# A fused cross-attention and FFN kernel: the maximum over the partitions by TensorE, first loads as units of the lists, new lists, and every second piece of w1 and w2 rounded by ScalarE

## The reference

```
n = layernorm(x)
q = quantized_linear(n, wq, bq)          # rows of n and rows of wq rounded to 127 levels by their own maximum
k = ctx @ wk.T + bk ; v = ctx @ wv.T + bv
o = softmax(q k.T / sqrt(32) + mask) v   # 16 heads of 32
x = x + quantized_linear(o, wo, bo)
n = layernorm(x)
h = gelu(quantized(n) @ quantized(W1).T * scales + B1)     # W1 and W2: one maximum over the WHOLE weight
x = x + quantized(h) @ quantized(W2).T * scales + B2
```

## Time and profile before

| what | us |
|---|---|
| median of three runs (lowest, highest) | 703.0 (701.41, 705.25) |
| the profiled execution, its own time | 699.67 |
| its span in the profile | 697.9 |
| PE busy | 639.8 (92%) |
| DVE busy | 475.1 (68%) |
| ACT busy | 462.5 (66%) |
| POOL busy | 219.0 (31%) |

### The profile page before, as it was taken

How to read it: one execution, slowest core, us unless ns; L and a number is a source line. 1 busy time by engine, 2 the same in 40 slices (tenths; PEclk the granted TensorE clock), 3 DMA queues, 4 the chain that set the end, 5 groups by cost and what they waited for, 6 DMA issues and landing times.

```text
span 697.9 us, 14934 instructions
## 1 busy us (share of the span) xinstructions
PE 639.8 (92%) x5168; PEld 475.6 (68%) x5168; DVE 475.1 (68%) x1173; ACT 462.5 (66%) x1158; POOL 219.0 (31%) x457
## 2 busy tenths in 40 slices
PE   2773996989999999999899999989999999999989
PEld 1562775857777687777777778767677776767644
DVE  4653884678667776778567563658577677878775
ACT  3241574658767776778578796668687867878812
POOL 0113330434071424235232433323424435221200
PEclk8896998999999999999999999999999999999999
DMA  9762596650605351353516352432533333232110
GB/s 307 273 92 58 65 263 129 157 157 19 84 24 98 94 75 27 58 105 23 132 10 113 79 66 23 71 75 33 59 97 67 79 49 61 40 58 41 39 38 23
DMA packets 80586, 58.67 MB, mean 84 GB/s; under 512 B 57984, under 2 KB 67968, under 8 KB 79872
## 3 DMA queue, kind: packets, MB, share of 16 engines
q1 hardware_dynamic: 80512, 57.72, 40.8%
HBM read 41.85 MB, written 3.68 MB: 65 GB/s over the span
## 4 chain that ended last, share of the span: by engine, by line
PE 72%; DVE 9%; DMA 9%; issue 5%; POOL 2%; ACT 2%; SPq 1%; DVEq 0%; POOLq 0%
PE ps_ring L1054 30%; PE ps_t L1088 11%; PE ps_ring L1160 7%; PE ps_s L1081 6%; PE ps_ring L1173 6%; PE ps_t L1100 5%; DMA rs_in<-row_sum 3%; PE ps_s L1149 3%; DMA oqT<-o_q 2%; PE ps_ring L1122 2%; PE ps_ring L1047 2%; DMA hT<-h_q 1%; DMA h<-in_wq 1%; DMA q_dram<-cols 1%; DVE cols L838 1%
## 5 line engine op out<-in xcount | busy, mean ns | idle before, releaser
L716 ACT ACTIVATE probs<-probs,neg_max 112x375 f32<-112x375 f32 x256 | 153.6, 602 | 42.7 <-DVE neg_max L867 42.1
L867 DVE CUSTOM_DVE_ANT_0 probs<-ps_s,mask_in 112x375 f32<-112x375 f32 x256 | 129.3, 545 | 60.0 <-PE ps_s L1081 51.8
L726 ACT ACTIVATE pT<-ps_t 125x336 f32<-125x336 f32 x256 | 110.2, 446 | 66.9 <-PE ps_t L1088 63.9
L1088 PEld LDWEIGHTS ps_t<-ident,probs 112*125 112x125 f32 x768 | 108.4, 189 | 40.2 <-issue 21.2
L1088 PE MATMUL ps_t<-ident,probs 112*125 112x112 f32 x768 | 120.5, 279 | 3.3 <-ACT pT L726 1.5
L1054 PE MATMUL ps_ring<-ctx_hi,wk_hi 128*128 128x376 f32 x256 | 91.9, 359 | 12.8 <-DVE ctx_lo L956 11.9
L1054 PE MATMUL ps_ring<-wv_hi,ctx_hi 128*125 128x512 f32 x192 | 80.5, 419 | 16.9 <-POOL ctx_lo L635 10.4
L1054 PE MATMUL ps_ring<-ctx_lo,wk_hi 128*128 128x376 f32 x256 | 86.8, 339 | 0.0
L1054 PE MATMUL ps_ring<-ctx_hi,wk_lo 128*128 128x376 f32 x256 | 86.8, 339 | 0.0
L635 POOL TENSOR_TENSOR ctx_lo<-ctx_in,ctx_hi 128x376 fp32r<-128x376 f32 x60 | 59.5, 997 | 74.3 <-ACT ctx_hi L694 52.8
L1054 PE MATMUL ps_ring<-wv_lo,ctx_hi 128*125 128x512 f32 x192 | 76.5, 398 | 0.0
(11 more groups left out here) (127 smaller groups left out, 1072.8 us busy)
## 6 DMA issues: line engine op xcount, KB each, us to landing
ctx_in<-in_ctxT SPq DMA_DIRECT2D x32, 375.0 KB, 5.0
h<-in_w2T SPq DMA_DIRECT2D x4, 1024.0 KB, 6.6
b_row<-in_w2T SPq DMA_DIRECT2D x4, 1024.0 KB, 7.3
x_in<-in_x SPq DMA_DIRECT2D x16, 224.0 KB
xres<-in_x SPq DMA_DIRECT2D x14, 256.0 KB, 2.9
out<-y SPq DMA_DIRECT2D x14, 256.0 KB, 2.3
mask_in<-in_mask SPq DMA_DIRECT2D x16, 164.1 KB, 3.7
w_q<-in_w1T SPq DMA_DIRECT2D x2, 1024.0 KB, 8.8
```

The lines of the kernel that those rows point to most:

```text
L716: nc.scalar.activation(probs[:, hd % SP_RING, :], probs[:, hd % SP_RING, :], ACT.Exp, scale=-1.0, bias=neg_max[:, b % 2, hd:hd + 1], accum ...
L726: nc.scalar.activation(pT[0:LR, hd % PT_RING, :], att_bank("T", b, hd)[0:LR, 0:LC * N], ACT.Copy).then_inc(pT_s, 1)
L867: nc.vector.tensor_tensor_reduce(out=probs[:, hd % SP_RING, :], in0=ps_s[hd % HG][0:N, 0:L], in1=mask_in[:, b % 2, :], scale=-1.0, scalar= ...
L1088: last = nc.tensor.transpose(bank[0:LR, lc * N:(lc + 1) * N], probs[:, hd % SP_RING, lc * LR:(lc + 1) * LR], ident[0:N, 0:N])
```

## The change

- **Maximum over the partitions.** POOL's `prepare` with its all-reduce goes. PE's new unit `w_max which.0` transposes the column of 128 maxima into one row (a matmul with the identity), DVE's new unit `w_max` reduces the row to one number, and PE's `w_max which.1` spreads it over the partitions (a matmul with a row of ones). DVE's step 5 reads it there. Both PE units take a bank of the ring.
- **Rounding.** Pieces m = 1 and m = 3 of w1 and of w2 are rounded by ACT (steps 7, 8, 11, 12 leave DVE's list and enter ACT's): ACTIVATE Identity with a scale and +constant, then with -constant. SP's loads into the buffers wait for ACT's semaphore where ACT frees them.
- **First loads.** They are units of SP's list. x comes first, then half of ctx and of wk, then wq; the bias rows come tens of units later. `mask_load 0.0` and `xres_load 0.0` stand behind `ctx_load 2.0` and `2.1`, no longer right behind the first weights.
- **Warm units** are of 4 matmuls in place of 8; 12 of them stand ahead of `k 0.0` in place of 2, and 3 more among the first work in place of 2. 24 in place of 12 stand in the last part.
- **All five lists are new**, with the same units otherwise. The last tile's lists on DVE and ACT are as before.

The lists up to the first heads, before and after (the rest is left out here; it differs by moves of some units, at most some thirty places):

```diff
 SP_UNITS
-w_load 0.0 prepare 0.0 0.1 0.2 x_load 0.0 ctx_load 0.0 0.1 prepare 0.3 0.6 mask_load 0.0 xres_load 0.0 prepare 0.8 w_load 0.1
-ctx_load 1.0 mask_load 1.0 w_load 0.2 0.3 xs_out 0.0 ctx_load 1.1 x_T 0.0 x_load 1.0 xs_in 0.0 ctx_load 2.0 2.1 xs_out 1.0 x_load
+x_load 0.0 ctx_load 0.0 load_wk 0.0 prepare 0.0 load_wq 0.0 load_wk 0.1 ctx_load 0.1 load_col 0.0 load_wv 0.0 prepare 0.1 load_wv
+0.1 load_col 0.1 prepare 0.2 load_wo 0.0 w_load 0.0 ctx_load 1.0 w_load 0.1 xs_out 0.0 ctx_load 1.1 prepare 0.3 w_load 0.2 x_load
+1.0 x_T 0.0 prepare 0.6 xs_in 0.0 w_load 0.3 ctx_load 2.0 mask_load 0.0 ctx_load 2.1 xres_load 0.0 load_row 0.0 prepare 0.8
...
 POOL_UNITS
-x_norm 0.0 x_quant 0.0 split 1.0 1.1 prepare 0.4 split 1.2 1.3 q 0.0 x_norm 1.0 split 2.0 2.1 x_quant 1.0 residual 0.0 split 2.2
+x_norm 0.0 split 1.0 x_quant 0.0 split 1.1 1.2 1.3 q 0.0 x_norm 1.0 split 2.0 2.1 2.2 x_quant 1.0 x_norm 2.0 split 2.3 residual
...
 ACT_UNITS
-split 0.0 0.1 0.2 w_hi 0.0 split 0.3 w_hi 0.1 k 0.0 w_hi 0.2 0.3 v 0.0 0.1 w_evac 0.0 v 0.2 w_evac 0.1 so 0.0 w_evac 0.2 split 1.0
-w_evac 0.3 0.4 0.5 0.6 split 1.1 k 0.1 0.2 w_evac 0.7 split 1.2 1.3 k 0.3 split 2.0 v 1.0 split 2.1 v 1.1 S 0.0 0.1 split 2.2 k
+split 0.0 0.1 w_hi 0.0 0.1 split 0.2 0.3 w_hi 0.2 k 0.0 0.1 0.2 w_evac 0.0 0.1 0.2 w_hi 0.3 w_evac 0.3 split 1.0 1.1 k 0.3 v 0.0
+split 1.2 v 0.1 split 1.3 v 0.2 w_evac 0.4 0.5 split 2.0 v 1.0 w_evac 0.6 split 2.1 w_evac 0.7 S 0.0 v 1.1 split 2.2 S 0.1 T 0.0
+prepare 0.7 k 1.0 prepare 0.8 S 0.2 k 1.1 S 0.3 T 0.1 prepare 0.11 S 0.4 0.5 T 0.2 so 0.0 split 2.3 v 1.2 T 0.3 S 0.6 T 0.4
+prepare 0.12 k 1.2 T 0.5 S 0.7 k 1.3 T 0.6 PV 0.0 S 0.8 0.9 T 0.7 S 0.10 0.11 split 3.0 T 0.8 0.9 S 0.12 PV 0.1 T 0.10 S 0.13 0.14
...
 DVE_UNITS
-w_lo 0.0 split 0.0 w_lo 0.1 split 0.1 0.2 w_rows 0.0 0.1 0.2 split 0.3 x_norm 0.0 w_lo 0.2 0.3 w_rows 0.3 0.4 prepare 0.0 w_rows
-0.5 x_quant 0.0 prepare 0.1 0.2 0.3 0.4 0.5 0.6 q 0.0 x_norm 1.0 prepare 0.7 S 0.0 prepare 0.8 x_quant 1.0 S 0.1 0.2 0.3 prepare
+split 0.0 w_lo 0.0 x_norm 0.0 w_rows 0.0 split 0.1 w_lo 0.1 split 0.2 0.3 x_quant 0.0 w_lo 0.2 w_rows 0.1 0.2 0.3 w_lo 0.3 w_rows
+0.4 0.5 prepare 0.0 0.1 x_norm 1.0 q 0.0 prepare 0.2 0.3 S 0.0 x_quant 1.0 prepare 0.4 S 0.1 w_max 0.0 S 0.2 0.3 prepare 0.5 0.6
...
 PE_UNITS
-warm 0.0 0.1 k 0.0 warm 0.2 v 0.0 0.1 warm 0.3 w_T 0.0 v 0.2 so 0.0 w_T 0.1 0.2 0.3 0.4 0.5 0.6 k 0.1 0.2 w_T 0.7 k 0.3 q 0.0 v
-1.0 S 0.0 v 1.1 k 1.0 v 1.2 S 0.1 T 0.0 0.1 k 1.1 1.2 T 0.2 0.3 S 0.2 T 0.4 PV 0.0 T 0.5 0.6 q 1.0 T 0.7 S 0.3 T 0.8 0.9 k 1.3 T
+warm 0.0 0.1 0.2 0.3 0.4 0.5 0.6 0.7 0.8 0.9 0.10 0.11 k 0.0 0.1 0.2 w_T 0.0 warm 0.12 w_T 0.1 0.2 warm 0.13 w_T 0.3 k 0.3 v 0.0
+0.1 0.2 q 0.0 w_T 0.4 warm 0.14 w_T 0.5 v 1.0 w_T 0.6 S 0.0 w_T 0.7 v 1.1 w_max 0.0 T 0.0 w_max 0.1 k 1.0 1.1 S 0.1 T 0.1 so 0.0 v
...
```

The functions:

```diff
-            def prepare(which, step):
-                if step == 4:
-                    pool.wait_ge(w_max, 2 * which + 1)
-                    nc.gpsimd.partition_all_reduce(w_all[:, which:which + 1], w_rs[:, 8 + which:9 + which], P,
-                                                   bass.bass_isa.ReduceOp.max).then_inc(w_max, 1)
...
+            def prepare(which, step):
+
+                stages, w = ((st_w1, w1_q), (st_w2, w2_q))[which]
+                m, rounding = (step - 5) // 2, (step - 5) % 2
+                stage, inv = stages[m % len(stages)], w_rs[:, 10 + which:11 + which]
+                if not rounding:
+                    act.wait_ge(round_ready, 2)
+                    act.wait_ge(w_inv, which + 1)
+                    if which == 1:
+                        act.wait_ge(w_in[12 + m], 16)
+                    nc.scalar.activation(stage, stage, ACT.Identity, scale=inv, bias=round_up[:]).then_inc(w_round_act, 1)
+                else:
+                    act.wait_ge(w_round_act, 2 * which + m // 2 + 1)
+                    nc.scalar.activation(w[:, :, :].rearrange("p k n -> p (k n)")[:, m * F:(m + 1) * F], stage, ACT.Identity,
+                                         bias=round_down[:]).then_inc(w_quant_act, 1)
...
-                        dve.wait_ge(w_max, 2 * which + 2)
-                        nc.vector.tensor_scalar(col[:], w_all[:, which:which + 1], 1.0 / LEVELS, None, ALU.mult).then_inc(w_col, 1)
+                        dve.wait_ge(w_max_all, which + 1)
+                        nc.vector.tensor_scalar(col[:], bank_of("w_max", which, 1)[:, 0:1], 1.0 / LEVELS, None, ALU.mult).then_inc(w_col, 1)
...
+            def w_max_part(which, i):
+                dve.wait_ge(w_max_T, which + 1)
+                nc.vector.tensor_reduce(w_one[:, which:which + 1], bank_of("w_max", which, 0)[0:1, 0:P], AX.X, ALU.max).then_inc(w_max_row, 1)
...
+            def w_max_unit(which, i):
+
+                if i == 0:
+                    pe.wait_ge(w_max, which + 1)
+                    bank = ring_bank("w_max", which, 0)
+                    nc.tensor.matmul(bank[0:1, 0:P], w_rs[:, 8 + which:9 + which], ident[:], start=True, stop=True).then_inc(w_max_T, 1)
+                else:
+                    pe.wait_ge(w_max_row, which + 1)
+                    bank = ring_bank("w_max", which, 1)
+                    nc.tensor.matmul(bank[:, 0:1], ones[0:1, :], w_one[:, which:which + 1], start=True, stop=True).then_inc(w_max_all, 1)
...
-WARM = 8
+WARM = 4
```

More of the change, by code:

```diff
@@ L43 @@
[L43 to L50, removed]
@@ new lines @@
+residual 2.0 x_quant 5.0 split 5.3 x_norm 6.0 y_norm 2.0 split 6.0 q 5.0 split 6.1 6.2 x_quant 6.0 split 6.3 7.0 residual 3.0
+x_norm 7.0 split 7.1 7.2 y_norm 3.0 split 7.3 y_quant 2.0 3.0 residual 4.0 q 6.0 x_quant 7.0 y_norm 4.0 split 8.0 8.1 8.2 q 7.0
+x_norm 8.0 x_quant 8.0 split 8.3 residual 5.0 split 9.0 9.1 y_norm 5.0 x_norm 9.0 split 9.2 y_quant 4.0 q 8.0 x_quant 9.0 split
+9.3 y_quant 5.0 residual 6.0 x_norm 10.0 split 10.0 10.1 10.2 y_norm 6.0 y_quant 6.0 split 10.3 q 9.0 x_quant 10.0 residual 7.0
@@ new lines @@
+12.12 12.13 x_norm 14.0 S 12.14 12.15 up 9.0 9.1 9.2 9.3 q 13.0 S 13.0 gather 10.0 h_absmax 9.0 o_quant 10.0 S 13.1 13.2 h_absmax
+9.1 S 13.3 h_absmax 9.2 9.3 x_quant 14.0 h_quant 9.0 out_proj 10.0 S 13.4 y_norm 10.0 S 13.5 13.6 13.7 y_quant 10.0 S 13.8 13.9
+13.10 13.11 down 9.3 S 13.12 13.13 x_norm 15.0 S 13.14 up 10.0 10.1 S 13.15 q 14.0 up 10.2 h_absmax 10.0 up 10.3 h_absmax 10.1
+10.2 10.3 h_quant 10.0 S 14.0 gather 11.0 o_quant 11.0 S 14.1 14.2 14.3 14.4 14.5 out_proj 11.0 S 14.6 14.7 y_norm 11.0 x_quant
@@ L192 @@
+1.16 1.17 1.18 h_T 13.0 13.1 warm 1.19 down 13.0 13.1 13.2 13.3 warm 1.20 1.21 1.22 1.23
 """
@@ L218 @@
 RING_USES = [use for use in turns(PE_UNITS)
-             if use[0] in ("w_T", "so", "q", "k", "v", "gather", "o_T", "out_proj", "y_T", "up", "h_T") or use[0] == "down" and use[2] == 0]
+             if use[0] in ("w_T", "so", "w_max", "q", "k", "v", "gather", "o_T", "out_proj", "y_T", "up", "h_T") or use[0] == "down" and use[2] == 0]
 RING_AT = {use: n for n, use in enumerate(RING_USES)}
@@ L665, in y_quant @@
                 nc.gpsimd.tensor_tensor(y[b % 2], y[b % 2], b2_row[:], ALU.add).then_inc(y_b2_s, 1)
-            units = {"prepare": prepare, "x_norm": x_norm, "split": split_lo, "x_quant": x_quant, "q": q, "residual": residual,
+            units = {"x_norm": x_norm, "split": split_lo, "x_quant": x_quant, "q": q, "residual": residual,
                      "y_norm": y_norm, "y_quant": y_quant}
@@ L1175, in down @@
                     last.then_inc(down_pe, 1)
-            units = {"w_T": w_T, "so": so, "q": q, "k": k_unit, "v": v_unit, "S": S, "T": T, "PV": PV, "gather": gather,
+            units = {"w_T": w_T, "so": so, "w_max": w_max_unit, "q": q, "k": k_unit, "v": v_unit, "S": S, "T": T, "PV": PV, "gather": gather,
                      "o_T": o_T, "out_proj": out_proj, "y_T": y_T, "up": up, "h_T": h_T, "down": down, "warm": warm}
```

338 lines of the change are left out of this document (174 added, 164 removed).

## The result

The kernel after takes 694.14 us (median of 4 runs, 691.96 to 695.85), the kernel before beside it 702.3 us (701.41 to 705.25): ratio 0.9875, 95% interval 0.9833 to 0.9917. It is faster by 1.2%, and not by the 4.0% of the forecast; 694 lies above the range. The profiled execution took 691.96 us, its span is 689.7.

The account below looks back on a forecast made before the run. TensorE's own work was taken as the bound from 200 to 660 us, with the loss in gaps before about 130 us. Terms -28.2 -6.5 +1.5 +1.1 +4 = -28.1 from 703.0 gave 675 us, range 664 to 687.

Parts of the forecast that it names:

- First loads, and TensorE up to S 0.0: Front: k 0.0 starts at about 16 us, first scores S 0.0 at 42 instead of 70.18, minus 28.2 us.
- The second stop: Before scores S 1.2 at 119.84 us: replacing the second all-reduce removes idle and slow scores, minus 6.5 us.
- The maximum itself: Two tiny matmuls and a DVE reduction per maximum cost 0.8 us each, plus 1.5 us for both.
- Rounding by ACT: Eight pieces add 16.4 us to ACT, of which a quarter shows, plus 4 us; DVE's saved 10.1 us count nothing.
- SP's queue: Row loads, mask 1 and xres move behind the first work on SP's list and are needed later: no cost.
- The rest of the lists and the tail: New orders of all 16 batches, same work, TensorE 98% busy: zero, bounds minus 10.6 and plus 10 us.
- The sum: All terms over the whole kernel: minus 28.1 us from the median of 703.0, giving 675 us.
- The condition named for being wrong: Middle of the kernel: the forecast is wrong if TensorE has over 20 us of idle there.
- TensorE's waits for ACT's copies: The forecast is wrong if these waits grow by over 10 us.
- (e): Rival: in every tile out_proj waits for the transposed oqT, 35 us over 13 tiles, 710 us; chance 0.03.
- (b): Rival: ACT becomes the bound in batches 0 and 1, its whole 16.4 us shows, 687 us; chance 0.13.
- (c): Rival: the new orders also remove the later idle of 10.6 us, 664 us; chance 0.13.

Follow-up runs that it names:

- experiment 7: Kernel of experiment 1 with both maxima over the partitions made by POOL's all-reduce again, w_max units gone: 679.35 us, ratio 0.9737 against 0.9573.
- experiment 11: Kernel of experiment 5 with all pieces of w1 and w2 rounded by DVE again, none by ACT: 675.5 us, ratio 0.9629.
- experiment 5: After kernel with 12 units on SP's list moved ahead of six stores of x's scales, other lists unchanged: 667.95 us, ratio 0.9577.
- experiment 1: After kernel's lists up to about 188 us, from there each engine's remaining units in before's order: 668.69 us, ratio 0.9573.
- experiment 10: Before kernel with x_load and r_move moved ahead of the store of x's scales for batches 2 to 14: 698.24 us, ratio 0.9955.
- the four kernels: Experiment 1, experiment 5, and experiment 1 with either its loads moved ahead of the store or the store issued by ACT: ratios 0.952 to 0.958.

## Why the prediction was wrong, point by point

**First loads, and TensorE up to S 0.0: right.** k 0.0 was put at about 16 at full clock, it is 16.69 at full clock; S 0.0 at 42, it is 43.80. The term was -28.2 and is -26.4. The sum of the units gave 43.5, and 42 was taken.

**The second stop: right in kind.** The 5.8 us of the earlier trace rows are gone. In their place TensorE waits 2.35 us at 90.94, not for w2's reduction but for a bank of the ring that v_sb held, and goes on slowly: the scores behind it take 1.57 us for five matmuls.

**The maximum itself: right.** Its first use costs a wait of 0.82 us ahead of the transpose, as forecast, and DVE's part is small:

```profile
L853 DVE TENSOR_REDUCE w_stat<-ps_ring 1x1 f32<-1x128 f32 x2 | 0.6, 280 | 0.9 <-PE ps_ring L1076 0.9
```

Two tiny matmuls and 0.28 us of DVE took the place of an instruction whose two uses cost 11.5 us in experiment 7. The rule weighed in the prediction ("GPSIMD Engine Reference" of the Trainium skill, section "Engine selection": a reduction along the partitions goes to GPSIMD) does not hold here, for one column of maxima.

**Rounding by ACT: the busy time right, the price not.** The eight pieces were put at 2.05 us each, 16.4 together:

```profile
L770 ACT ACTIVATE b_row<-b_row,round_up,w_stat 128x2048 f32<-128x2048 f32 x3 | 6.3, 2099 | 2.0 <-DMA b_row<-in_w2T 1.5 <-DVE w_stat L838 0.5
...
L773 ACT ACTIVATE w_q<-b_row,round_down 128x2048 bf16<-128x2048 f32 x3 | 6.0, 1991 | 0.0
```

But they were to cost 4 us, with DVE's 10.1 us worth nothing, "off the path". Undone, they made the kernel no faster: 0.9914 against 0.9875, and 0.9629 against 0.9577 where no stop hides it. Both point the other way, a gain of some 3 us, and neither interval excludes zero. The stop of 3.76 us at 63.91 in experiment 11 shows one place where DVE's pieces were on the path after all: scores stand behind them.

**SP's queue: "Nothing", and "The rest of the lists and the tail: Zero, bounds minus 10.6 and plus 10": wrong, and this is the step that failed.** It was argued from 98% busy and from the same work per batch. That bounds what an order can win, not what it can lose. The bound of plus 10 had no row under it. What the order lost is 3.0 points, 21 us, by experiment 5, on six places of SP's list; by experiment 1, 3.0 points too. Of SP only what was moved in the front was followed, to the times at which DVE and POOL need it; which load stands behind which DMA in the rest of its list was not. A row for it was there, in before's own chain and in its timeline of SP:

```profile
325.81 9.18 DMA rs_in<-row_sum
```

```profile
324.92 0.32 SPq L536 DMA_DIRECT2D q_dram<-cols  x1
```

This rs_in takes 9.18 us to land, 0.89 us behind a store, where xres lands in 2.9 at the median. Before can afford it (experiment 10: at most 0.75% for x_in and rs_in together). In the new order TensorE soon needs what waits for just these loads, as the chains of the stops show.

**The sum.** Without this step it comes out: minus 28.1 us is 4.0%, and the after kernel with the 12 units moved measures 0.9577, minus 4.2%. That it is so close is in part luck, since errors cancel in it: the front gave 1.8 us less and the second stop kept 2.35 us, while the 4 us put on ACT's rounding were not paid. The condition named for being wrong, over 20 us of idle in the middle, was met with 22.5. So was, in name, another: TensorE's waits for ACT's copies of oT, pT, k_sb and v_sb grew from 4.8 to 16.3 us, but 7.0 of these are the stops at 319 and 437 us, which are no fault of ACT. The rivals missed it too: (e), the slower one, looked at the right kind of thing, a DMA that TensorE ends up waiting for in every tile, but at oqT's (0.2 us in after), not at those behind the store. ACT was not the bound (b), and the later idle was not removed but doubled (c).

**What stays open.** After without the store takes 658 us, 1.4 points under the same kernel with its loads ahead. The first leaves out the way of x's scales to q (`xs_in` no longer waits for the store) as well as the store's effect on the DMAs near it, and the two weren't separated. Nor was it tried what bounds the four kernels that come to a ratio of 0.952 to 0.958, or through what the store holds up the other DMAs.
